# Attention block over four batches on one core: unequal maxima units, a reordered batch end, the batch loop written out

## Chip, core and metric

One core of a Trainium2 chip runs the whole program. The metric is the device time of one execution in microseconds (us); the three timed executions before the change gave 4074.82, 4076.78 and 4077.01.

## What is computed

For each of 4 batches of x (512 channels, 48 × 48 = 2304 positions, float32):

```
xn   = groupnorm(x, 32 groups) * gn_w + gn_b
qkv  = qkv_w @ xn + qkv_b            # 8 heads of 64 channels
w    = softmax((q k) / 8)            # 2304 x 2304 per head
a    = w @ v
out  = xn + proj_w @ a + proj_b
```

## The kernel before

The engines run programs of their own and meet only by semaphores. The names: `B` = 4 batches, `PAIRS` = 4 pairs of heads, `CH` = 6 chunks of `N` = 384 positions, `KT` = 18 key tiles of 128. A step is one key tile against one chunk of queries for both heads of a pair; 18 steps are a block, 108 a pair, 432 (`BSTEPS`) a batch.

**The stream.** Steps go two by two (a slot, 54 per pair, 864 in all). TensorE's `stream` (L619) issues per slot: the maxima unit of the first step, the scores of both steps (`make_scores`, L538 to 559), the maxima unit of the second, projection work for later heads (`behind`, L593), and the values products of the slot before (`make_pv`, L568). q and k are kept as a rounded part and its rest (`q_hi`, `q_lo`, ...) of type fp32r, so scores take three products; the values and the q, k, v projections are plain fp32. Scores of even steps are added onto a seed that ScalarE copies into the bank (`seed`, L759), those of odd steps onto two seed matmuls (L553); the seed is the negated row maximum.

**Maxima units.** `max_unit` (L512) makes the scores of 128 queries against 384 keys for both heads into `aux_banks`, and VectorE's `unit_max` (L860) reduces them to one number per query and head. There is one pair of banks, so each unit waits for the reduction of the one before (`aux_done`, L515). Units run `AHEAD` = 24 steps ahead of their scores. After 18 units `negate_max` (L866) reduces and turns the maxima, and SyncE's `send_max` (L353) sends them through DRAM to the seeds.

**Other engines.** ScalarE: two exponentials per slot (`exponentials`, L749), the next seed, the rounded parts. GpSimd: `add` (L1075) sums the probabilities of a block in `denom`, 17 adds a block, each waiting for the exponential and for the add before. The ring of probabilities `probs` holds `RING` = 8 steps; an exponential waits until its place was read by the values product and by the add. After a block, `finish` (L529) sums over the partitions on TensorE, VectorE's `take_recip` (L938) turns this into reciprocals in four pieces and multiplies (L961), and SyncE stores the block to `att` (`put_block`, L368).

**Order of the projection work.** `batch_plan` (L66) places the q, k, v work by hand: in the inner pairs 8 of the 9 slots of a block hold some, in the last pair 20 of 54 do, among them the next batch's first k, q and v. The next batch's x is loaded, its statistics and normalization are made in the last pair; `coefs` (L920) is a chain of small VectorE operations. The last batch has none of this.

**The end of a batch** ("seam"). TensorE ends `stream` with the last values products and the `finish` of the last block, which waits for the last add (L531). Then `projection` (L641): for each of 6 chunks, 48 matmuls of 384 columns (rounded part with both parts of the weights, then the rest), in the four score banks. `att_in` holds two chunks; `load_att` (L411) of chunk tc + 2 waits for the projection of chunk tc. ScalarE rounds a chunk (`att_high`, L743, 1536 columns), VectorE subtracts in place (`att_low`, L963), ScalarE copies each result out of the bank (L814), VectorE adds xn (L1022), SyncE stores the chunk and then loads the next x chunk into its place. `xres` and `proj_sb` lie in `probs`. The next batch's ScalarE part begins with a wait for both last stores (L840) and then seeds step 0. `batch` runs in a hardware loop (`Fori`) for batches 0 to 2; batch 3 is written out.

Of the kernel before, what the change touches and what calls it, by code (L numbers as in the profile page):

```python
# [5 lines left out]
def attention_block_program(nc, x, gn_w, gn_b, wqkv_t, bqk, bv, wproj_t, bproj, att, out):  # L6
# [17 lines left out]
    N = 384  # L24
# [21 lines left out]
    AHEAD = KT + 6  # L46
    EARLY_Q = 2
# [13 lines left out]
    NORM_AT, NORM_EVERY = 33, 2  # L61

# [101 lines left out]
    with ExitStack() as ctx:  # L164
# [27 lines left out]
        att_in = [sb(f"att_in{i}", [128, CT, N], fp32r) for i in range(2)]  # L192
# [7 lines left out]
        spare = sb("spare", [128, 1])  # L200
        small = sb("small", [128, 64])
# [12 lines left out]

        def head(e):
            return slice(e * D, (e + 1) * D)
# [9 lines left out]

        def xres(i):
            return probs[:, CT * N * i:CT * N * (i + 1)].rearrange("p (o n) -> p o n", n=N)

        proj_sb = probs[:, 2 * CT * N:4 * CT * N].rearrange("p (o n) -> p o n", n=N)  # L230
        att_hi = [buf[:, 0:CT * N].rearrange("p (k n) -> p k n", n=N)
                  for buf in (k_hi[(PAIRS - 1) % 2], k_lo[(PAIRS - 1) % 2])]
# [62 lines left out]
        def first_batch(k):  # L295
            return isinstance(k, int)
# [40 lines left out]
        def _(sp):  # L337
# [15 lines left out]
            def send_max(n, blk):  # L353


                par = blk % 2
                sp.wait_ge(neg_ready, n + 1)
                for i in range(4):
                    sp.dma_start(neg_rows[:, 32 * i:32 * (i + 1)],
                                 neg_cols[32 * i:32 * i + 2 * QT, :]).then_inc(neg_out, 16)  # L360
                sp.wait_ge(neg_out, 64 * (n + 1))
                if not isinstance(n, int) or n >= 2:
# [11 lines left out]
            def stream(b, last):  # L374
                before, _ = PLANS[last]
                nb = b + 1
                for s in range(BSTEPS):
# [18 lines left out]
                    if s in PUT_AT:  # L396
                        put_block(b, PUT_AT[s])
# [13 lines left out]
            def load_att(b, tc):  # L411
                i = tc % 2
                sp.dma_start(att_in[i][:, :, :].bitcast(fp32), att[:, :, chunk(tc)]
                             .rearrange("k c t -> c k t")).then_inc(att_back[i], 16)
# [4 lines left out]
            def projection(b):  # L419
                sp.wait_ge(att_out, PRIMED + 16 * (BLOCKS * b + BLOCKS - 1))  # L420
                load_att(b, 0)
                load_att(b, 1)
                put_block(b, BLOCKS - 1)

                for tc in range(2):
                    if tc == 1:
                        sp.wait_ge(att_out, PRIMED + 16 * BLOCKS * (b + 1))
# [36 lines left out]
            with sp.Fori(0, B - 1) as b:  # L464
                batch(b, False)
            batch(B - 1, True)
# [11 lines left out]
        def _(pe):  # L478
            mm = nc.tensor.matmul

            def bank_for(u):

                if not isinstance(u[1], int) or u[1] > 0:
                    pe.wait_ge(bank_free[u[0]], u[1])
                return bank(u)
# [26 lines left out]
            def max_unit(n, p, qt, kc):  # L512

                if not isinstance(n, int) or n > 0:
# [104 lines left out]
            def stream(b, last):  # L619
# [17 lines left out]
                finish(b, BLOCKS - 1, use(b, last, TAIL))  # L637
                if not last:
                    wait_free(pe, use(b, last, ("v", PAIRS, VG - 1)))

            def projection(b):  # L641

                pe.wait_ge(wproj_lo_ready, 1)
                for tc in range(CH):
                    i = tc % 2
                    for low in range(2):
                        pe.wait_ge(att_lo_ready if low else att_hi_ready, CH * b + tc + 1)
                        products = ([(wproj_hi, att_in[i])] if low
                                    else [(wproj_hi, att_hi[i]), (wproj_lo, att_hi[i])])
                        for ot in range(CT):  # L650
# [3 lines left out]
                            for w, a in products:  # L654
                                for k in range(CT):
                                    last = mm(scores[:, n // 2 % 2, n % 2, 0:N], w[:, k, ot * 128:(ot + 1) * 128],  # L656
                                              a[:, k, :], start=(not low and w is wproj_hi and k == 0),
                                              stop=(low == 1 and k == CT - 1))
                            if low:
                                last.then_inc(proj_full, 1)  # L660
# [39 lines left out]
            def batch(b, last):  # L700
                stream(b, last)
                projection(b)

            with pe.Fori(0, B - 1) as b:
                batch(b, False)
            batch(B - 1, True)
# [3 lines left out]
        def _(act):  # L710
# [32 lines left out]
            def att_high(b, tc):  # L743
# [3 lines left out]
                a(att_hi[i], att_in[i][:, :, :].bitcast(fp32), ACT.Copy).then_inc(att_hi_ready, 1)  # L747

            def exponentials(s, b):  # L749

                if s >= RING:
# [7 lines left out]
            def seed(s, b):  # L759
# [4 lines left out]
                if s < 2:  # L764
                    act.wait_ge(banks_opened, 1)
                    act.wait_ge(proj_saved, PRIMED + PJ * b)
# [17 lines left out]
            def stream(b, last):  # L784
                before, after = PLANS[last]
                seed(0, b)
# [16 lines left out]
                att_high(b, 0)  # L803
                save_o(b, BLOCKS - 1)

            def projection(b):
# [31 lines left out]
            def batch(b, last):  # L838
                for i in range(2):
                    act.wait_ge(stored[i], PRIMED + 16 * (CH // 2) * b)  # L840
                stream(b, last)
                projection(b)

            with act.Fori(0, B - 1) as b:
                batch(b, False)
            batch(B - 1, True)
# [3 lines left out]
        def _(dve):  # L850
# [9 lines left out]
            def unit_max(n, qt, kc, rows_negated):  # L860
# [3 lines left out]
                v.tensor_reduce(maxima[:, :, qt, kc], aux_banks[:, :, 0:N], AX.X, ALU.max).then_inc(aux_done, 1)  # L864
# [98 lines left out]
            def att_low(b, tc):  # L963

                i = tc % 2
                dve.wait_ge(att_hi_ready, CH * b + tc + 1)
                v.tensor_tensor(att_in[i][:, :, :], att_in[i][:, :, :].bitcast(fp32), att_hi[i].bitcast(fp32),
                                ALU.subtract).then_inc(att_lo_ready, 1)
# [25 lines left out]
            def stream(b, last):  # L994
# [12 lines left out]
                att_low(b, 0)  # L1007
                for piece in range(PIECES):
                    take_recip(b, BLOCKS - 1, use(b, last, TAIL), piece)

            def projection(b):
                att_low(b, 1)
# [42 lines left out]
            def batch(b, last):  # L1055
# [8 lines left out]
                projection(b)  # L1064

            with dve.Fori(0, B - 1) as b:
                batch(b, False)
            batch(B - 1, True)
# [3 lines left out]
        def _(pool):  # L1072
# [33 lines left out]
            with pool.Fori(0, B - 1) as b:  # L1106
                batch(b)
            batch(B - 1)
# [37 lines left out]
```

## Time and profile before

| | |
|---|---|
| median of three executions | 4076.78 us |
| the profiled execution | 4077.72 us, span 4076.0 us |
| mean granted TensorE clock | 0.988 |
| TensorE, VectorE, ScalarE, GpSimd busy | 97%, 54%, 57%, 74% |
| instructions | 84658 |

Times in the rows are in us from the start of the span; durations of one instruction marked ns are in nanoseconds. PE is TensorE's matmul side and PEld its weight loads, DVE is VectorE, ACT ScalarE, POOL GpSimd. A matmul's record ends where the profiler models its end, so overlapping records are a pipeline; the distance between starts is the pace. In brackets behind an instruction stand the idle time of its engine before it and what ended it.

### The profile page before, as it was taken

How to read it: one execution, taken by the hardware profiler on the slowest of the kernel's cores; microseconds unless marked ns; L12 is line 12 of the kernel's file. 1: busy time of each engine (PE TensorE's matmuls, PEld its weight loads, DVE VectorE, ACT ScalarE, POOL GpSimd, SP SyncE). 2: the span in 40 equal slices, each digit the busy share in tenths (PEclk: the TensorE clock that was granted, in tenths of full speed). 3: DMA queues.
4: the chain of work that ended last, by engine and by line, in shares of the span. 5: the costliest groups of instructions: out<-in, count | busy, mean ns of one | idle time of the engine just before them, and what ended most of it. 6: DMA issues, size and time to landing. Idle time of an engine off the chain costs nothing.

```text
span 4076.0 us, 84658 instructions
## 1 busy us (share of the span) xinstructions
PE 3933.8 (97%) x31730; PEld 2472.5 (61%) x31730; DVE 2217.9 (54%) x2809; ACT 2308.0 (57%) x3159; POOL 3004.5 (74%) x1639
## 2 busy tenths in 40 slices
PE   6999999999899999999989999999999999999997
PEld 3566665656656566565665656566567565656656
DVE  4555555565455555566545555556644555555552
ACT  2555555565455555556535555555654555555563
POOL 0778878777288888877728888887773888888893
PEclk9999999999999999999999999999999999999999
DMA  2000000120400000012130000002113000000004
GB/s 74 16 20 24 18 22 21 43 87 18 148 19 18 22 22 20 20 57 73 39 131 18 22 21 16 24 20 75 59 43 121 21 16 21 22 18 19 19 19 144
DMA packets 133751, 165.87 MB, mean 41 GB/s; under 512 B 61648, under 2 KB 110800, under 8 KB 132816
## 3 DMA queue, kind: packets, MB, share of 16 engines
q1 hardware_dynamic: 133328, 160.26, 12.5%
q8 instruction: 262, 4.29, 0.4%
q14 instruction: 161, 1.32, 0.1%
HBM read 122.17 MB, written 38.04 MB: 39 GB/s over the span
## 4 chain that ended last, share of the span: by engine, by line
PE 88%; issue 4%; DVE 3%; POOL 3%; DMA 2%; SPq 0%; ACT 0%; POOLq 0%; DVEq 0%; ACTq 0%
PE oacc L577 26%; PE scores L557 20%; PE pool_bank L495 13%; PE aux_banks L517 13%; PE pool_bank L507 7%; PE scores L656 3%; PE scores L553 3%; POOL denom L1087 3%; PE pool_bank L534 2%; DMA att_in<-att 1%; DVE maxima L864 1%; DVE turned L945 1%; DMA out<-probs 1%; PE scores L495 1%; PE scores L507 0%
## 5 line engine op out<-in xcount | busy, mean ns | idle before, releaser
L1087 POOL TENSOR_TENSOR denom<-denom,probs 128x768 f32<-128x768 f32 x1536 | 2829.3, 1842 | 568.3 <-ACT probs L756 473.3
L864 DVE TENSOR_REDUCE maxima<-aux_banks 128x2 f32<-128x768 f32 x1728 | 1657.2, 959 | 1389.1 <-PE aux_banks L517 1379.4
L756 ACT ACTIVATE probs<-scores 128x768 f32<-128x768 f32 x1728 | 1347.2, 812 | 1259.2 <-PE scores L557 1253.2
L577 PE MATMUL oacc<-probs,vals 128*64 128x384 f32 x6912 | 1277.0, 491 | 0.0
L517 PE MATMUL aux_banks<-k_hi,q_hi 64*128 64x384 f32 x3456 | 762.5, 437 | 43.2 <-DVE maxima L864 39.2
L577 PEld LDWEIGHTS oacc<-probs,vals 128*64 128x64 f32 x6912 | 471.1, 137 | 503.9 <-issue 466.8
L517 PEld LDWEIGHTS aux_banks<-k_hi,q_hi 64*128 64x128 f32 x3456 | 323.2, 184 | 693.2 <-issue 451.2
L769 ACT ACTIVATE scores<-seeds 128x768 f32<-128x768 f32 x864 | 700.1, 810 | 4.3 <-DMA out<-probs 4.3
L557 PE MATMUL scores<-q_hi,k_hi 64*128 64x384 f32 x3456 | 587.3, 335 | 22.7 <-ACT scores L769 22.6
L557 PE MATMUL scores<-q_lo,k_hi 64*128 64x384 f32 x3456 | 588.6, 335 | 0.0
L557 PE MATMUL scores<-q_hi,k_lo 64*128 64x384 f32 x3456 | 585.6, 334 | 0.0
L1084 POOL TENSOR_TENSOR denom<-probs 128x768 f32<-128x768 f32 x96 | 174.6, 1819 | 442.1 <-ACT probs L756 442.1
L557 PEld LDWEIGHTS scores<-q_hi,k_hi 64*128 64x128 f32 x3456 | 327.4, 186 | 33.9 <-ACT scores L769 32.7
L557 PEld LDWEIGHTS scores<-q_lo,k_hi 64*128 64x128 f32 x3456 | 328.0, 185 | 0.0
L557 PEld LDWEIGHTS scores<-q_hi,k_lo 64*128 64x128 f32 x3456 | 327.3, 185 | 0.0
L495 PE MATMUL pool_bank<-xn,wq 128*64 128x384 f32 x1504 | 293.2, 505 | 1.6
L553 PE MATMUL scores<-seeds,shares 64*128 64x384 f32 x1728 | 292.7, 334 | 0.0
L507 PE MATMUL pool_bank<-wv,xn 128*64 128x128 f32 x4416 | 287.9, 277 | 1.8
L495 PE MATMUL pool_bank<-xn,wk 128*64 128x384 f32 x1456 | 281.4, 501 | 1.9
L507 PEld LDWEIGHTS pool_bank<-wv,xn 128*64 128x64 f32 x4416 | 236.9, 137 | 42.9 <-issue 36.6
L553 PEld LDWEIGHTS scores<-seeds,shares 64*128 64x128 f32 x1728 | 163.2, 185 | 0.0
L495 PEld LDWEIGHTS pool_bank<-xn,wq 128*64 128x64 f32 x1504 | 90.1, 137 | 103.1 <-issue 96.8
(91 smaller groups left out, 1681.3 us busy)
## 6 DMA issues: line engine op xcount, KB each, us to landing
seeds<-neg_rows SPq DMA_DIRECT2D x96, 384.0 KB, 3.5
xtile<-x SPq DMA_DIRECT2D x72, 384.0 KB, 3.2
att<-o_norm SPq DMA_DIRECT2D x96, 192.0 KB, 1.9
att_in<-att SPq DMA_DIRECT2D x24, 768.0 KB, 6.3
probs<-x SPq DMA_DIRECT2D x24, 768.0 KB, 4.7
out<-probs SPq DMA_DIRECT2D x24, 768.0 KB, 5.2
neg_rows<-neg_cols SPq DMA_DIRECT2D x384, 0.8 KB
xn<-x SPq DMA_DIRECT2D x4, 1152.0 KB, 8.6
```

The costliest lines, as they stand in the source:

```text
L495: last = mm(to[head(e), 0:N], w[:, k, head(e)], xn[:, k, chunk(c)], start=(k == 0), stop=(k == CT - 1))
L507: last = mm(to[head(half), i * 128:(i + 1) * 128], xn[:, k, t0:t0 + D], wv[:, k, :], start=(k == 0), stop=(k == CT - 1))
L517: last = mm(aux_banks[:, e, 0:N], q_hi[head(e), qt * 128:(qt + 1) * 128], k_hi[p % 2][head(e), chunk(kc)], start=True, stop=True)
L553: mm(slot[:, e, :], shares[head(e), :], seeds[blk % 2][head(e), e * N:(e + 1) * N], start=True, stop=False)
L557: last = mm(slot[:, e, :], ks[head(e), keys], qs[head(e), queries], start=False, stop=(n == 2), skip_group_check=(s % 2 == 0))
L577: ins = mm(oacc[head(e), 0:N], vals[p % 2][:, kt, head(e)], prob(s)[:, e * N:(e + 1) * N], start=(kt == 0), stop=(kt == KT - 1))
L656: last = mm(scores[:, n // 2 % 2, n % 2, 0:N], w[:, k, ot * 128:(ot + 1) * 128], a[:, k, :], start=(not low and w is wproj_hi and k == 0), ...
L756: a(prob(s).rearrange("p (h n) -> p h n", n=N), scores[:, s % 2, :, 0:N], ACT.Exp, scale=SCALE).then_inc(probs_ready, 1)
L769: a(scores[:, 0, :, 0:N], seeds[blk % 2][:, :].bitcast(fp32).rearrange("p (e n) -> p e n", n=N), ACT.Copy).then_inc(seeded, 1)
L864: v.tensor_reduce(maxima[:, :, qt, kc], aux_banks[:, :, 0:N], AX.X, ALU.max).then_inc(aux_done, 1)
L1084: gp.tensor_tensor(acc, prob(s - 1), prob(s), ALU.add).then_inc(added, 1)
L1087: gp.tensor_tensor(acc, acc, prob(s), ALU.add).then_inc(added, 1)
```

## The change

What it does:

- The maxima units alternate between 320 and 448 keys (`UNIT_KEYS`) where they had 384 each; a slot's first unit has 320, its second 448. Their number is the same.
- `att_in` (two buffers, split in place) becomes raw, rounded and rest buffers of their own: raw chunk 0 in the x tile, raw chunk 1 new, rounded and rest of even chunks new, those of odd chunks in `k_hi` and `k_lo`.
- Chunks 0 and 1 are loaded back when block 20 of the batch is stored, chunk 2 after block 22. Chunk 0 is split in four parts of 384 columns in slots 43 to 46 (ScalarE) and 44 to 47 (VectorE) of the last pair. Later loads wait for the split of the chunk two before.
- TensorE projects chunk 0 before the last block's `finish`. ScalarE's first eight copies wait for the adds that still read their places. `proj_sb` and `xres` change places in `probs`; the x loads wait for the last add and values product.
- ScalarE seeds step 0 of the next batch between the copies of results 21 and 22; the wait for the stores moves to step 4, step 0 waits for the last output instead. A one-element exponential stands at the start of a batch.
- All engines run the four batches as a straight program.

The diff, cut to its core:

```
+    UNIT_KEYS = (320, 448)
+    SPLIT_AT = 43
...
+        def unit_keys(kc):
+            start = kc // 2 * sum(UNIT_KEYS) + kc % 2 * UNIT_KEYS[0]
+            return slice(start, start + UNIT_KEYS[kc % 2])
...
+        proj_sb = probs[:, 0:2 * CT * N].rearrange("p (o n) -> p o n", n=N)
         def xres(i):
+            return probs[:, CT * N * (2 + i):CT * N * (3 + i)].rearrange("p (o n) -> p o n", n=N)
+        att_raw = [four(xtile[:, :, :].rearrange("p a b -> p (a b)")), att_raw1[:, :, :]]
+        att_hi = [att_hi0[:, :, :], four(k_hi[last_keys])]
+        att_lo = [att_lo0[:, :, :], four(k_lo[last_keys])]
...
@@ SyncE, stream
+                        if blk == BLOCKS - 4:
+                            sp.wait_ge(xn_ready, XITEMS * (b + 1 if last else b + 2))
+                            sp.wait_ge(att_out, PRIMED + 16 * (BLOCKS * b + blk + 1))
+                            load_att(b, 0)
+                            load_att(b, 1)
+                        elif blk == BLOCKS - 2:
+                            sp.wait_ge(att_out, PRIMED + 16 * (BLOCKS * b + blk + 1))
+                            load_next_att(b, 0)
...
+            def load_next_att(b, tc):
+                sp.wait_ge(att_lo_ready, CT * (CH * b + tc + 1))
+                load_att(b, tc + 2)
@@ SyncE, projection
-                sp.wait_ge(att_out, PRIMED + 16 * (BLOCKS * b + BLOCKS - 1))
-                load_att(b, 0)
-                load_att(b, 1)
-                put_block(b, BLOCKS - 1)
+                sp.wait_ge(pv_done, PRIMED + BSTEPS * (b + 1))
+                sp.wait_ge(added, PRIMED + ADDS * BLOCKS * (b + 1))
                 for tc in range(2):
                     sp.dma_start(xres(tc), chan(x, b, tc)).then_inc(xres_in[tc], 16)
                 for tc in range(CH):
-                    if tc + 2 < CH:
-                        sp.wait_ge(proj_full, PJ * b + CT * (tc + 1))
-                        load_att(b, tc + 2)
+                    if tc == 2:
+                        sp.wait_ge(att_out, PRIMED + 16 * BLOCKS * (b + 1))
+                    if tc + 3 < CH:
+                        load_next_att(b, tc + 1)
+                    if tc == 0:
+                        put_block(b, BLOCKS - 1)
@@ TensorE
-                    last = mm(aux_banks[:, e, 0:N], q_hi[head(e), qt * 128:(qt + 1) * 128],
-                              k_hi[p % 2][head(e), chunk(kc)], start=True, stop=True)
+                    last = mm(aux_banks[:, e, 0:UNIT_KEYS[kc % 2]], q_hi[head(e), qt * 128:(qt + 1) * 128],
+                              k_hi[p % 2][head(e), unit_keys(kc)], start=True, stop=True)
...
                 for tc in range(CH):
+                    if tc == 1:
+                        finish(b, BLOCKS - 1, use(b, last, TAIL))
@@ ScalarE
             def exponentials(s, b):
+                if s == 0:
+                    act.wait_ge(out_ready, PRIMED + PJ * b)
+                if s == RING // 2:
+                    for i in range(2):
+                        act.wait_ge(stored[i], PRIMED + 16 * (CH // 2) * b)
...
+                    n = i - (PAIRS - 1) * SLOTS - SPLIT_AT
+                    if 0 <= n < CT:
+                        att_high(b, 0, slice(n, n + 1))
...
+                    else:
+                        act.wait_ge(added, PRIMED + ADDS * BLOCKS * (b + 1) - (RING - 1 - n // 2))
                     a(proj_sb[:, n % 8, :], ...
+                    if n == PJ - 3 and not last:
+                        seed(0, b + 1, PRIMED + PJ * b + n + 1)
...
             def batch(b, last):
-                for i in range(2):
-                    act.wait_ge(stored[i], PRIMED + 16 * (CH // 2) * b)
+                a(warm[:, :], ones[:, 0:1], ACT.Exp)
@@ VectorE, stream
+                    n = i - (PAIRS - 1) * SLOTS - SPLIT_AT - 1
+                    if 0 <= n < CT:
+                        att_low(b, 0, slice(n, n + 1))
@@ every engine
-            with pe.Fori(0, B - 1) as b:
-                batch(b, False)
-            batch(B - 1, True)
+            for b in range(B):
+                batch(b, b == B - 1)
```

## Rows read from the trace of the kernel before

**Rows 1.** The page, part 1: busy us (share of span) xinstructions.

```profile
PE 3933.8 (97%) x31730; PEld 2472.5 (61%) x31730; DVE 2217.9 (54%) x2809; ACT 2308.0 (57%) x3159; POOL 3004.5 (74%) x1639
```

**Rows 2.** Windows, two pairs: stretch, us, PE, PEld, DVE, ACT, POOL busy, PEclk, DMA.

```profile
563.00:793.00 230.00, 229.72 (x1910) 140.27 (x1908) 127.56 (x157) 136.05 (x186) 187.40 (x102) 1.00 0.07 20
3341.60:3572.20 230.60, 229.78 (x1910) 141.09 (x1910) 127.70 (x157) 132.87 (x187) 187.14 (x102) 1.00 0.07 20
```

**Rows 3.** Time line, batch 3, slot without projection work: start us, us.

```profile
3930.20 0.18 PEld L517 LDWEIGHTS aux_banks<-k_hi,q_hi 64*128 64x128 f32 x2 [0.60 <-DVE maxima L864]
...
3930.69 0.96 DVE L864 TENSOR_REDUCE maxima<-aux_banks 128x2 f32<-128x768 f32 x1 [0.86 <-PE aux_banks L517]
...
3931.29 1.51 ACT L756 ACTIVATE probs<-scores 128x768 f32<-128x768 f32 x2 [1.09 <-PE scores L557]
...
3931.36 0.19 PEld L557 LDWEIGHTS scores<-q_lo,k_hi 64*128 64x128 f32 x2
3931.53 0.34 PE L557 MATMUL scores<-q_lo,k_hi 64*128 64x384 f32 x2
3931.70 0.19 PEld L517 LDWEIGHTS aux_banks<-k_hi,q_hi 64*128 64x128 f32 x2 [0.16 <-DVE maxima L864]
...
3932.07 1.51 PE L577 MATMUL oacc<-probs,vals 128*64 128x384 f32 x8
3932.18 0.96 DVE L864 TENSOR_REDUCE maxima<-aux_banks 128x2 f32<-128x768 f32 x1 [0.54 <-PE aux_banks L517]
...
3932.70 0.81 ACT L769 ACTIVATE scores<-seeds 128x768 f32<-128x768 f32 x1
...
3933.51 0.19 PEld L517 LDWEIGHTS aux_banks<-k_hi,q_hi 64*128 64x128 f32 x2 [0.60 <-DVE maxima L864]
```

**Rows 4.** Time line of the first seam, and the last batch's end.

```profile
1040.28 1.55 PE L534 MATMUL pool_bank<-denom,ones 128*64 128x384 f32 x4 [4.38 <-POOL denom L1087]
...
1098.27 0.44 PE L517 MATMUL aux_banks<-k_hi,q_hi 64*128 64x384 f32 x2 [0.94 <-ACT probs L814]
...
1103.98 1.28 ACT L769 ACT_TABLE_LOAD   x1 [6.04 <-DMA out<-probs]
...
4015.84 1.55 PE L534 MATMUL pool_bank<-denom,ones 128*64 128x384 f32 x4 [12.13 <-POOL denom L1087]
```

**Rows 5.** Windows, after the first seam, and the last projection.

```profile
1106.10:1110.50 4.40, 4.36 (x22) 3.11 (x24) 0.96 (x1) 2.33 (x3) 0.81 (x1) 0.50 0.00 0
4022.10:4070.80 48.70, 48.40 (x275) 47.28 (x273) 19.32 (x27) 18.09 (x28) 0.00 (x0) 1.00 0.71 239
```

**Rows 6.** Time line of TensorE in the last slots of batch 3, without units.

```profile
3997.43 0.35 PE L557 MATMUL scores<-q_lo,k_hi 64*128 64x384 f32 x2
...
3997.72 1.51 PE L577 MATMUL oacc<-probs,vals 128*64 128x384 f32 x8
...
4000.64 0.34 PE L557 MATMUL scores<-q_lo,k_hi 64*128 64x384 f32 x2
...
4000.91 0.54 PE L577 MATMUL oacc<-probs,vals 128*64 128x384 f32 x2
```

**Rows 7.** By source line: duration ns min/median/max, start of first, last.

```profile
L869 DVE TENSOR_REDUCE neg_max<-maxima x96: 190/191/192, 86.9 to 3958.3; 128x6 fp32r<-128x36 f32 x96
L961 DVE TENSOR_TENSOR o_norm<-o_raw,recip x96: 547/1360/2223, 159.9 to 4018.9; 128x384 f32<-128x384 f32 x96
```

**Rows 8.** Time line of GpSimd, in the loop and in batch 3.

```profile
568.48 3.73 POOL L1087 TENSOR_TENSOR denom<-denom,probs 128x768 f32<-128x768 f32 x2 [2.04 <-ACT probs L756]
...
3929.89 5.78 POOL L1087 TENSOR_TENSOR denom<-denom,probs 128x768 f32<-128x768 f32 x3
```

**Rows 9.** Time line, a product L961 in a slot without projection work.

```profile
3890.55 2.11 DVE L961 TENSOR_TENSOR o_norm<-o_raw,recip 128x384 f32<-128x384 f32 x1
...
3893.58 0.44 PE L517 MATMUL aux_banks<-k_hi,q_hi 64*128 64x384 f32 x2 [0.92 <-DVE maxima L864]
```

**Rows 10.** The page, DMA issues: out<-in, count, KB each, us to landing.

```profile
out<-probs SPq DMA_DIRECT2D x24, 768.0 KB, 5.2
```

More of the change, by code:

```diff
@@ L191, in attention_block_program @@
         wproj_lo = sb("wproj_lo", [128, CT, C], fp32r)
-        att_in = [sb(f"att_in{i}", [128, CT, N], fp32r) for i in range(2)]
+        att_hi0 = sb("att_hi0", [128, CT, N], fp32r)
+        att_lo0 = sb("att_lo0", [128, CT, N], fp32r)
+        att_raw1 = sb("att_raw1", [128, CT, N])
         groups = sb("groups", [128, 128])
@@ L481, in bank_for @@
             def bank_for(u):
-                if not isinstance(u[1], int) or u[1] > 0:
+                if u[1] > 0:
                     pe.wait_ge(bank_free[u[0]], u[1])
@@ L636, in stream, with projection @@
                 make_pv(BSTEPS - 1, b, last)
[L637 to L641, printed above, removed]
+            def projection(b, last):
                 pe.wait_ge(wproj_lo_ready, 1)
@@ L645, in projection @@
                     i = tc % 2
+                    if tc == 1:
+                        finish(b, BLOCKS - 1, use(b, last, TAIL))
+                        if not last:
+                            wait_free(pe, use(b, last, ("v", PAIRS, VG - 1)))
                     for low in range(2):
-                        pe.wait_ge(att_lo_ready if low else att_hi_ready, CH * b + tc + 1)
-                        products = ([(wproj_hi, att_in[i])] if low
+                        pe.wait_ge(att_lo_ready if low else att_hi_ready, CT * (CH * b + tc + 1))
+                        products = ([(wproj_hi, att_lo[i])] if low
                                     else [(wproj_hi, att_hi[i]), (wproj_lo, att_hi[i])])
@@ L655, in projection @@
                                 for k in range(CT):
-                                    last = mm(scores[:, n // 2 % 2, n % 2, 0:N], w[:, k, ot * 128:(ot + 1) * 128],
-                                              a[:, k, :], start=(not low and w is wproj_hi and k == 0),
-                                              stop=(low == 1 and k == CT - 1))
+                                    ins = mm(scores[:, n // 2 % 2, n % 2, 0:N], w[:, k, ot * 128:(ot + 1) * 128],
+                                             a[:, k, :], start=(not low and w is wproj_hi and k == 0),
+                                             stop=(low == 1 and k == CT - 1))
                             if low:
-                                last.then_inc(proj_full, 1)
+                                ins.then_inc(proj_full, 1)
             pe.sem_inc(pv_done, PRIMED)
@@ L701, in batch @@
                 stream(b, last)
-                projection(b)
-            with pe.Fori(0, B - 1) as b:
-                batch(b, False)
-            batch(B - 1, True)
+                projection(b, last)
+            for b in range(B):
+                batch(b, b == B - 1)
         @block.scalar
@@ L757, in exponentials, with seed @@
                   scale=SCALE).then_inc(probs_ready, 1)
-            def seed(s, b):
+            def seed(s, b, since=None):
                 blk = s // KT
@@ L765, in seed @@
                     act.wait_ge(banks_opened, 1)
-                    act.wait_ge(proj_saved, PRIMED + PJ * b)
+                    act.wait_ge(proj_saved, since)
                 else:
@@ L838, in batch @@
             def batch(b, last):
-                for i in range(2):
-                    act.wait_ge(stored[i], PRIMED + 16 * (CH // 2) * b)
+                a(warm[:, :], ones[:, 0:1], ACT.Exp)
                 stream(b, last)
[L842 to L846, printed above, removed]
+                projection(b, last)
+            act.wait_ge(consts_made, 5)
+            seed(0, 0, PRIMED)
+            for b in range(B):
+                batch(b, b == B - 1)
         @block.vector
@@ L1063, in batch @@
                 stream(b, last)
[L1064 to L1068, printed above, removed]
+                projection(b, last)
+            for b in range(B):
+                batch(b, b == B - 1)
         @block.gpsimd
@@ L1104, in batch @@
                     add(s, b)
-            with pool.Fori(0, B - 1) as b:
+            for b in range(B):
                 batch(b)
-            batch(B - 1)
 def kernel(**inputs):
```

48 lines of the change are left out of this document (22 added, 26 removed).

## The prediction, made before the change was run

> **What bounds the kernel now.** The page first: TensorE is busy in 97% of the span [rows 1], so time can only come from what stands between its matmuls. Then the windows, one pair of heads each: in 230.6 us of an undisturbed pair it is busy 229.8 [rows 2]. It looks full, but a matmul that waits for its weights counts as busy, so the time line of one pair of steps has to be read [rows 3], a "slot" from here on. It holds two maxima units (L517), two score steps and two steps of values, 3.31 us in all. The second unit's weight load starts at 3931.70, 0.05 after the reduction of the first unit ends (3930.69 + 0.96). Other loads start 0.17 ahead of their matmul, as the one at 3931.36 for 3931.53 does; the unit's would have started at about 3931.53. So VectorE's reduction of unit one is late by 0.17 us for the load, and part of that shows on TensorE. Last I read the ends of the batches: windows and time line of the seam [rows 4, 5].
>
> **Units of 320 and 448 keys.** From the last scores pair to the first values pair there are 0.54 us with a unit between (3931.53 to 3932.07) [rows 3]; without one it is 0.29 and 0.27 [rows 6]. A unit's pair itself takes 0.17, so 0.08 to 0.10 are lost per slot; I take 0.09. The reduction takes 0.96 us for 768 values [rows 3] and 0.191 for 36 [rows 7], 1.05 ns a value. An estimate by that slope: 0.83 for 640 values, 1.09 for 896. The first unit's matmuls also end 0.03 sooner (64 of 384 columns of 0.17). Together 0.16 of the missing 0.17: the load is back in its place to 0.01. The total of columns stays the same. Bounds: below nothing if the reduction does not shrink with its width, 0.17 at most, the whole lateness.
> What is late next is unit one of the next slot, behind the reduction of 896. In the slot without projection work the reduction now ends at 3932.18 + 0.96 = 3933.14, the load starts at 3933.51 [rows 3]: 0.37 spare, of which 0.05 is the signal. The new reduction is 0.13 longer, its matmuls end 0.03 later but start 0.09 sooner, and the slot is 0.09 shorter: some 0.17 stays. ScalarE's chain is as close: exp, exp, seed from 3931.29 to 3933.51 [rows 3], and the scores behind unit one want the seed about 0.1 after 3933.51. At most this eats some of the 0.09 in slots without projection work, one in nine in the inner pairs.
> How many slots: 12 inner pairs of 54 are 648; the last pairs of batches 0 to 2 add 162; the last pair of batch 3 counts with its first 9 only, since GpSimd bounds the rest. 819 × 0.09 = 74 us.
> The Trainium skill (TensorE: Matmul & The Clock Gate, Part 3, The mechanism) has it that a weight load overlaps a running matmul only where the row groups differ; both halves are in use by the scores in front, so by that rule the 0.09 would stay. That is rival A, 4028 us in full. The trace speaks against it: loads on the same halves run 0.17 ahead all through the slot.
>
> **Straight program.** Batch 3 already is one, and its pair takes 230.6 us by the windows against 230.0 and a little in the loops (the windows are cut at tenths; I take 0.45 more in the straight one), with the same work [rows 2]. 9 pairs × 0.45 = +4 us. GpSimd loses more: two adds in the loop span 3.73, three in the straight batch 5.78 [rows 8]; with 1.83 each (half of 3.73 less the gap) the gap goes from 0.08 to 0.14. 17 adds then take 33.5 us against 37.5 of a block: hidden. But VectorE's product L961, two inputs from SBUF, takes 1.36 in the median and 0.55 at least [rows 7]; I read the difference as the wait until an add is over. GpSimd loses its 0.2 of idle time a slot, so the product may end up to 0.2 later, with about 0.1 left until it delays unit one's reduction. 96 blocks × 0 to 0.1, taken as +5 us.
>
> **The seam.** TensorE stops at 1035.90 (1040.28 − 4.38, waiting for the sums) and makes its first scores at 1106.1, when the table load at 1103.98 and the seed behind it (0.81) are over [rows 4]: 70.2 us. In the new order projection chunk 0 follows at once, its data split before the end; the sums' finish stands behind it. Its matmuls go at 48.40/275 = 0.176 us with the missing records [rows 5], so 288 take 50; the finish 0.65 at full clock. A chunk is 8.3 us, GpSimd's lag about 4.3 + 1 (its wider gaps) + 1 (less TensorE time): just covered; without this cover TensorE waits for it behind chunk 0. Then unit one waits for the last copy, 0.9 after the last matmul group began to end [rows 4], + 0.7 since the next seed (0.81) now stands in ScalarE's queue before the last two copies, + 0.3 to the scores. 52.5 us against 70.2: 17.7. The loads of the attention chunks now wait for the split of the chunk two before, not for its projection, so their landing and split are hidden behind 8.3; SyncE passes a store and its 5.2 us [rows 10] before each, which still fits. The x loads start later, at the sums' end, and the outputs with them; 8 buffers of results take that up. Stores (ScalarE's 6.04 wait at 1103.98) are now waited for at step 4, some 8 us into the batch, where they are hidden; the table load of 1.28 goes too [rows 4]. Where batch 3 begins that load is absent already: 1.3 less. So 17.7 × 3 − 1.3 = 52 us. The clock: behind the idle time the granted clock was 0.50, half of 2.4 GHz, in 1106.1 to 1110.5 [rows 5], 2.2 us lost; without a pause it should stay up, 3 × 2 = 6 us. Seams: 58 us.
>
> **Added before the seam.** The split of chunk 0 is now four copies and four subtractions in the last slots, which have no projection work. ScalarE has 1.09 us idle in each [rows 3], a copy needs half of that. The subtraction, of the form of L961, does not fit: in such a slot L961 took 2.11 and TensorE lost 0.92 [rows 9]. 4 × 3 batches × 0.75 = +9 us (0 to 13). In the last batch no units run there any more. SyncE's new waits at the 21st and 23rd block are for work done some ten steps before; the row maxima queued behind them are sent more than 20 steps ahead of their use.
>
> **The last seam.** TensorE waits 12.13 us for the sums, until 4015.84 [rows 4], and GpSimd's chain is unchanged. Chunk 0 (8.3) now runs in that wait: −8. The program's first seed, too, needs no table load (1.28): −1.
>
> **Sum.** −74 + 4 + 5 − 58 + 9 − 8 − 1 = −123. The profiled execution took 4077.7 us (span 4076.0), 0.9 over the median: 4077.7 − 123 − 0.9 = 3954 us.
>
> **Rivals.**
> A. The units give nothing: load not pulled ahead, or ScalarE's chain paces. For: every unit load of [rows 3] waits, none shows the other case. Against: the scores loads. 3954 + 74 = 4028 in full; half, 3991. Chance 0.12.
> B. The seam is not bound by matmuls: SyncE's queue (x load, attention load, store, wait) paces it as now, 1 to 2 us per chunk, or the sums come late behind chunk 0. 3 × 8 = 24 us back: 3978. For: one queue carries all of it. Against: each load has a chunk's time more. Chance 0.12.
> C. Slower. The reduction of 896 holds unit one in every slot. It decides from 0.17 us beyond my 1.09 in bare slots, about 0.8 in the others. To turn 123 − 8 us it would have to cost 0.15 to 0.2 in each of 852 slots, so take some 2 us: 4077 + 10 = 4087. Against: the slope of [rows 7]. Chance 0.02.
> D. The product of L961 slips by a whole add in each block: up to 0.92 [rows 9] × 72 = 66 us, 4020. Chance 0.06.
> The forecast itself has 0.68. Its own range is 3930 to 3975: 0.08 to 0.10 per slot (±8), the subtractions (−9, +4), L961 (±5), seams ±6.
>
> **How the numbers follow.** The likeliest case gives 3954. The range takes in B and half of A: 3925 to 3992; outside are full A, C, D and a little luck below. About 0.2% (8 us) can be told from no change. Faster 0.96, same 0.02, slower 0.02.
>
> **What would show it.** The window of an inner pair at 225 to 226 us; the load of the second unit 0.17 ahead of its matmul, and 0.27 to 0.29 from unit to values; reductions of 0.83 and 1.09; GpSimd's gaps 0.14 everywhere; 52 to 54 us from the last values to the next scores, granted clock 1.00 across; a table load only around the square roots and before the first exponential. It is wrong if the pair stays at 230, if TensorE waits for attention data within a seam, or if unit one waits for the wide reduction.

## The result, and the profile after

The changed kernel takes 3937.84 us in the median of four runs (3936.28 to 3938.25), against 4076.9 for the kernel before: a ratio of 0.9657 (95% interval 0.9641 to 0.9674), 139 us less. The forecast was 3954 us, in a range of 3925 to 3992.

The page of the changed kernel, part 1, against [rows 1]: TensorE's share rises by one point only, but for the same 31730 matmuls it is busy for 3842.4 us where it was 3933.8: a matmul that waits for its weights counts as busy. With equal units and all else changed (below) it is 3919.1, so 77 of these 91 us go with the units.

```profile
PE 3842.4 (98%) x31730; PEld 2451.3 (62%) x31730; DVE 2223.0 (56%) x2821; ACT 2275.7 (58%) x3173; POOL 3002.6 (76%) x1639
```

Windows of an inner pair after, in the columns of [rows 2]: 225.0 us where it was 230, for the same instructions.

```profile
1200.00:1425.00 225.00, 224.63 (x1912) 139.58 (x1910) 127.58 (x157) 132.98 (x187) 187.25 (x103) 1.00 0.07 21
```

The time line of a slot without projection work, batch 3, against [rows 3]:

```profile
3756.27 0.19 PEld L546 LDWEIGHTS aux_banks<-k_hi,q_hi 64*128 64x128 f32 x2 [0.60 <-DVE maxima L904]
...
3756.73 0.83 DVE L904 TENSOR_REDUCE maxima<-aux_banks 128x2 f32<-128x640 f32 x1 [0.56 <-PE aux_banks L546]
...
3757.34 1.51 ACT L791 ACTIVATE probs<-scores 128x768 f32<-128x768 f32 x2 [1.01 <-PE scores L586]
...
3757.41 0.19 PEld L586 LDWEIGHTS scores<-q_lo,k_hi 64*128 64x128 f32 x2
...
3757.58 0.34 PE L586 MATMUL scores<-q_lo,k_hi 64*128 64x384 f32 x2
3757.61 0.19 PEld L546 LDWEIGHTS aux_banks<-k_hi,q_hi 64*128 64x128 f32 x2
3757.76 0.36 PE L546 MATMUL aux_banks<-k_hi,q_hi 64*128 64x448 f32 x2
...
3758.05 1.51 PE L606 MATMUL oacc<-probs,vals 128*64 128x384 f32 x8
3758.16 1.09 DVE L904 TENSOR_REDUCE maxima<-aux_banks 128x2 f32<-128x896 f32 x1
...
3758.75 0.82 ACT L804 ACTIVATE scores<-seeds 128x768 f32<-128x768 f32 x1
...
3759.48 0.19 PEld L546 LDWEIGHTS aux_banks<-k_hi,q_hi 64*128 64x128 f32 x2 [0.60 <-DVE maxima L904]
```

The first reduction (640 values) takes 0.83 us and ends at 3757.56, the load follows 0.05 later, at 3757.61, 0.15 ahead of its matmuls at 3757.76. The matmuls keep the pace of the scores (3757.58 to 3757.76), and the values follow after 0.29 where it was 0.37, though this pair is 64 columns wider. The slot takes 3.21 us, not 3.31. The load is still released by the reduction: counted over the 852 slots that hold units, the second unit's load starts 0.05 us behind the reduction's end in the median, in the changed kernel as before, and 0.15 behind it in the kernel with 256 keys first (below). It is only no longer late enough to matter.

Windows of the first seam and of its edge, against [rows 5], and the time line, against [rows 4]:

```profile
1011.00:1067.00 56.00, 54.54 (x316) 51.70 (x318) 25.66 (x33) 22.97 (x33) 8.92 (x5) 1.00 0.62 200
1066.30:1075.00 8.70, 7.45 (x58) 4.55 (x60) 5.78 (x11) 5.04 (x8) 3.65 (x2) 1.00 0.37 133
```

```profile
1013.62 0.96 PE L686 MATMUL scores<-att_hi,wproj_hi 128*128 128x384 f32 x4
...
1022.14 0.87 PE L563 MATMUL pool_bank<-denom,ones 128*64 128x384 f32 x4
...
1061.09 7.40 SPq L465 DMA_DIRECT2D out<-probs  x2
...
1061.89 2.94 PE L686 MATMUL scores<-k_lo,wproj_hi 128*128 128x384 f32 x16
...
1064.45 0.81 ACT L804 ACTIVATE scores<-seeds 128x768 f32<-128x768 f32 x1 [0.39 <-ACT probs L852]
...
1066.29 0.42 PE L546 MATMUL aux_banks<-k_hi,q_hi 64*128 64x320 f32 x2 [1.46 <-ACT probs L852]
...
1066.54 0.33 PE L586 MATMUL scores<-q_hi,k_hi 64*128 64x384 f32 x2
...
1068.12 1.51 ACT L791 ACTIVATE probs<-scores 128x768 f32<-128x768 f32 x2 [1.79 <-DVE probs L1065]
```

Chunk 0 starts as the last values product ends, the finish (L563) stands behind it without a wait, and the scores start at 1066.54: 52.9 us from the end of the values (1013.69) where it was 70.2. The granted clock is 1.00 over both windows. The last two stores land 7.40 us after 1061.09; nothing waits for them. The first exponential waits 1.79 us for VectorE's last output, whose x chunk comes late. TensorE has its first scores by then, but the reduction of the first unit stands behind that output too, and the second unit waits for it:

```profile
1069.20 0.47 PE L546 MATMUL aux_banks<-k_hi,q_hi 64*128 64x448 f32 x2 [1.25 <-DVE maxima L904]
```

Time line of the last seam, and the window over it. Chunk 0 ends and the finish still waits for GpSimd, 2.88 us by the row where it was 12.13 [rows 4]; the granted clock stays at 1.00 in this execution.

```profile
3881.48 2.94 PE L686 MATMUL scores<-att_lo,wproj_hi 128*128 128x384 f32 x16
...
3887.30 0.87 PE L563 MATMUL pool_bank<-denom,ones 128*64 128x384 f32 x4 [2.88 <-POOL denom L1129]
```

```profile
3884.00:3892.00 8.00, 5.12 (x29) 4.20 (x28) 1.95 (x4) 2.29 (x3) 3.10 (x2) 1.00 0.44 138
```

### The profile page after: what moved, and what is told of

Read it like the earlier page. It is cut to its first block, busy times and chain, and to the rows that moved or that the text cites. A ratio compares the mean times of both kernels' runs of the same rounds, so it can differ in the third digit from the quotient of the medians.

```text
span 3936.0 us, 77117 instructions
## 1 busy us (share of the span) xinstructions
PE 3842.4 (98%) x31730; PEld 2451.3 (62%) x31730; DVE 2223.0 (56%) x2821; ACT 2275.7 (58%) x3173; POOL 3002.6 (76%) x1639
## 4 chain that ended last, share of the span: by engine, by line
PE 66%; POOL 4%; DVE 2%; DMA 1%; issue 1%; ACT 0%; POOLq 0%; SPq 0%; DVEq 0%; ACTq 0%
PE oacc L606 20%; PE scores L586 16%; PE pool_bank L524 10%; PE aux_banks L546 8%; PE pool_bank L536 5%; POOL denom L1129 3%; PE scores L582 3%; PE scores L686 2%; PE pool_bank L563 1%; DMA out<-probs 1%; DVE maxima L904 1%; DMA probs<-x 0%; ACT probs L791 0%; DVE probs L1065 0%; DVE att_lo L1008 0%
## 5 line engine op out<-in xcount | busy, mean ns | idle before, releaser
L904 DVE TENSOR_REDUCE maxima<-aux_banks 128x2 f32<-128x640 f32 x1728 | 1657.9, 959 | 1318.3 <-PE aux_banks L546 1288.9
L791 ACT ACTIVATE probs<-scores 128x768 f32<-128x768 f32 x1728 | 1310.8, 810 | 1247.3 <-PE scores L586 1231.2
L546 PE MATMUL aux_banks<-k_hi,q_hi 64*128 64x448 f32 (+1 forms) x3456 | 683.4, 391 | 41.2 <-DVE maxima L904 35.0
```

The lines of the kernel that those rows point to most:

```text
L546: last = mm(aux_banks[:, e, 0:UNIT_KEYS[kc % 2]], q_hi[head(e), qt * 128:(qt + 1) * 128], k_hi[p % 2][head(e), unit_keys(kc)], start=True, ...
L791: a(prob(s).rearrange("p (h n) -> p h n", n=N), scores[:, s % 2, :, 0:N], ACT.Exp, scale=SCALE).then_inc(probs_ready, 1)
L904: v.tensor_reduce(maxima[:, :, qt, kc], aux_banks[:, :, 0:UNIT_KEYS[kc % 2]], AX.X, ALU.max)\
```

## The experiments

All times are medians of four or more runs; kernels of one group ran on the same chip with the kernel before, which gave 4078.25, 4079.76 and 4079.88 us in the three groups.

### Equal units in the changed kernel

```
-    UNIT_KEYS = (320, 448)
+    UNIT_KEYS = (384, 384)
```

> The changed kernel with equal units (384 and 384) again, all else changed. Theory: a slot loses the 0.10 us that the trace after shows regained (0.697 + 0.542 against 0.667 + 0.470), in some 810 slots: 3938 + 83 = 4021 us, inner pairs back at 230.2, the second unit's load 0.17 behind the last scores matmul. Rival (the straight program, with waits on constants, brings most of the pair's gain): 3945 to 3960 us, pairs at 226.

Measured: 4015.8 us (ratio 0.9845, 0.9828 to 0.9861). Inner pair, in windows:

```profile
551.00:781.70 230.70, 229.88 (x1910) 141.16 (x1908) 127.79 (x156) 132.99 (x187) 187.23 (x103) 1.00 0.07 20
```

The units are worth 4015.8 − 3936.7 = 79 us; the second number is the changed kernel in the second group, which ran on another chip (the kernel before differs by 1.5 us between the two). The rival falls.

### Unequal units in the kernel before

```
+    UNIT_KEYS = (320, 448)
-    last = mm(aux_banks[:, e, 0:N], q_hi[...], k_hi[p % 2][head(e), chunk(kc)], ...)
+    last = mm(aux_banks[:, e, 0:UNIT_KEYS[kc % 2]], q_hi[...], k_hi[p % 2][head(e), unit_keys(kc)], ...)
-    v.tensor_reduce(maxima[:, :, qt, kc], aux_banks[:, :, 0:N], ...)
+    v.tensor_reduce(maxima[:, :, qt, kc], aux_banks[:, :, 0:UNIT_KEYS[kc % 2]], ...)
```

> The kernel before, with units of 320 and 448 keys alone. Theory: inner pairs at 224.9 in the loops too, 4077 - 83 = 3994 us, seams as before (70 us). Rival (the units need the other parts): less than half of it, above 4035 us.

Measured: 3999.04 us (ratio 0.9803, 0.9787 to 0.9820), 79 us again, in loops:

```profile
551.00:775.50 224.50, 224.50 (x1912) 138.87 (x1910) 127.50 (x157) 136.07 (x187) 187.82 (x103) 1.00 0.07 21
```

The gain does not depend on the rest, and the pair is 0.5 us shorter than in the changed kernel. TensorE is busy in all of it.

### The straight program alone

```
-            with pe.Fori(0, B - 1) as b:
-                batch(b, False)
-            batch(B - 1, True)
+            for b in range(B):
+                batch(b, b == B - 1)
```
(on every engine; `first_batch(k)` becomes `k == 0`)

> The kernel before, with the four batches written out alone. Theory as predicted: pairs 230.2 to 230.6 (up to +4 us in sum), two table loads of 1.3 us and the branch fewer at the seams: 4074 to 4079 us, no change that can be told; GpSimd's gaps 0.14 in all batches. Rival (the 16 us by which the result beat the forecast come from here): 4058 to 4065 us.

Measured: 4074.43 us (ratio 0.9991, 0.9981 to 1.0000), 3.8 us less than the kernel before of its group. Its inner pairs take 230.7 us, 0.5 more, as forecast (9 × 0.5 = +4.5); its later seams 67.6 and 67.5 from values to scores where they took 70.0 and 68.8 before. One more thing differs: once a batch, in batches 0 to 2, TensorE stands behind the chain of small VectorE operations of `coefs`, for 5.64 to 5.68 us before and for 3.80 here and 3.84 in the changed kernel.

```profile
867.25 0.69 PE L517 MATMUL aux_banks<-k_hi,q_hi 64*128 64x384 f32 x2 [5.64 <-DVE maxima L864]
```

In this kernel:

```profile
866.25 0.69 PE L516 MATMUL aux_banks<-k_hi,q_hi 64*128 64x384 f32 x2 [3.80 <-DVE maxima L861]
```

GpSimd's two adds, against [rows 8]:

```profile
567.81 3.80 POOL L1083 TENSOR_TENSOR denom<-denom,probs 128x768 f32<-128x768 f32 x2 [2.06 <-ACT probs L754]
```

3.80 − 3.73 = 0.07 us more between two adds. The longer pairs and the shorter seams nearly cancel.

### 448 keys first

```
-    UNIT_KEYS = (320, 448)
+    UNIT_KEYS = (448, 320)
```
(and the first units wait for one k chunk more)

> The changed kernel with the order of widths turned: 448 first, 320 second. Theory (the first unit's reduction prices the slot, one to one once it is late): against equal units the first reduction is 0.13 us longer and its matmuls end 0.03 later, so 0.16 more in each of some 810 slots: 4021 + 130 = 4151 us, pairs at 238.9. Rival (the width matters little; the balance of both units counts): within 15 us of equal units, 4010 to 4035 us.

Measured: 4128.62 us (ratio 1.0122, 1.0105 to 1.0139). The time line of units and reductions:

```profile
1300.46 0.47 PE L546 MATMUL aux_banks<-k_hi,q_hi 64*128 64x448 f32 x2
...
1300.98 1.09 DVE L904 TENSOR_REDUCE maxima<-aux_banks 128x2 f32<-128x896 f32 x1 [0.37 <-PE aux_banks L546]
...
1302.12 0.41 PE L546 MATMUL aux_banks<-k_hi,q_hi 64*128 64x320 f32 x2
...
1302.58 0.83 DVE L904 TENSOR_REDUCE maxima<-aux_banks 128x2 f32<-128x640 f32 x1 [0.51 <-PE aux_banks L546]
```

Between the units there are 1.66 us, where 1.49 stand in the changed kernel (3756.27 to 3757.76). A pair takes 238.0 us, 7.3 over equal units: 0.135 a slot, not 0.16. The theory forgot that the second unit's matmuls then are 0.027 shorter; 0.16 − 0.027 = 0.13. Late widths are priced one to one, and the order alone moves the kernel by 192 us.

### 256 and 512 keys

```
-    UNIT_KEYS = (320, 448)
+    UNIT_KEYS = (256, 512)
```

> The changed kernel with units of 256 and 512 keys. Theory: the first reduction is early enough with 320 already, so nothing more is won there, and the wide reduction (1024 values, 1.23 us) still ends before unit one's load, whose spare falls from 0.18 to about 0.03 us: 3938 us, within 4. Rival (rival C of the prediction: the wide reduction holds unit one in slots without projection work, and there the products behind it hurt more): 3945 us or more.

Measured: 3935.18 us (ratio 0.9646, 0.9629 to 0.9663), the changed kernel within the noise. By source line, the reductions of this kernel:

```profile
L904 DVE TENSOR_REDUCE maxima<-aux_banks x1728: 628/956/1229, 43.1 to 3823.6; 128x2 f32<-128x512 f32 x96, 128x2 f32<-128x1024 f32 x96
```

They now last up to 1.229 us, and inner pairs take 224.7 instead of 224.9. Time line of the first reduction and the second unit's load:

```profile
3755.15 0.69 DVE L904 TENSOR_REDUCE maxima<-aux_banks 128x2 f32<-128x512 f32 x1
...
3755.99 0.19 PEld L546 LDWEIGHTS aux_banks<-k_hi,q_hi 64*128 64x128 f32 x2
```

The load is 0.17 ahead of its matmuls (3756.16) and 0.15 behind the reduction's end, so it no longer waits for it. The pair is 0.3 us shorter than with 320 keys, 0.005 a slot, for the last 0.03 of lateness. So 320 was early enough. Behind the wide reduction no first unit is held, here or in the changed kernel: past the program's start the load of none follows the reduction's end by less than 0.06 us. Rival C's mechanism has no price even at 1024 values.

### The changed kernel again

As the reference for the second group:

> The changed kernel itself, as the reference of this group. 3938 us again, within 0.1%.

Measured: 3936.68 us (ratio 0.9649, 0.9633 to 0.9665).

### The split of chunk 0 six slots earlier

```
-    SPLIT_AT = 43
+    SPLIT_AT = 37
```

> The changed kernel with the four-part split of chunk 0 six slots earlier (slots 37 to 41), of which all but one hold projection work. Theory: the subtractions no longer delay unit one's reduction, so the last pairs of batches 0 to 2 shorten by what the split costs, forecast 3 us each, by the trace rather 2: 3938 - 6 = 3932 us. Rival (the split is hidden as it is): 3938 us.

Measured: 3933.93 us (3931.70 to 3935.99) against 3936.68 (3935.24 to 3938.31) for the changed kernel in the same group: 2.8 us, hardly clear of the spread. Time line of the changed kernel in slots 44 to 47:

```profile
980.61 0.80 DVE L1008 TENSOR_TENSOR att_lo<-xtile,att_hi 128x384 fp32r<-128x384 f32 x1
...
983.84 1.66 DVE L1008 TENSOR_TENSOR att_lo<-xtile,att_hi 128x384 fp32r<-128x384 f32 x1
...
986.29 0.48 PE L546 MATMUL aux_banks<-k_hi,q_hi 64*128 64x448 f32 x2 [0.48 <-DVE maxima L904]
...
987.82 1.75 DVE L1008 TENSOR_TENSOR att_lo<-xtile,att_hi 128x384 fp32r<-128x384 f32 x1
...
990.36 0.47 PE L546 MATMUL aux_banks<-k_hi,q_hi 64*128 64x448 f32 x2 [0.59 <-DVE maxima L904]
...
991.88 1.73 DVE L1008 TENSOR_TENSOR att_lo<-xtile,att_hi 128x384 fp32r<-128x384 f32 x1
```

Two of the four subtractions delay the next unit by 0.48 and 0.59 us, and by 0.45 to 0.59 in batches 1 and 2. In the earlier slots no unit behind them has such a wait in these three batches. In the last batch, where slots 37 to 41 still hold units, two have, of 0.58 and 2.66 us; the pair, which GpSimd bounds, takes 198.0 us all the same, between the 199.1 and 197.0 of the changed kernel's two executions. Time line of the last batch, earlier split:

```profile
3824.95 2.16 DVE L1008 TENSOR_TENSOR att_lo<-xtile,att_hi 128x384 fp32r<-128x384 f32 x1
...
3827.90 0.47 PE L546 MATMUL aux_banks<-k_hi,q_hi 64*128 64x448 f32 x2 [2.66 <-DVE maxima L904]
```

The last pairs of batches 0 to 2 are 3.6 us shorter in sum than in the changed kernel of the group; more than that was forecast (6) and is not there.

### The split in one piece at the end

```
-                    n = i - (PAIRS - 1) * SLOTS - SPLIT_AT
-                    if 0 <= n < CT:
-                        att_high(b, 0, slice(n, n + 1))
+                att_high(b, 0)
                 save_o(b, BLOCKS - 1)
```
(the same on VectorE; chunk 2 is then loaded at the seam)

> The changed kernel with chunk 0 split in one piece behind the last slot. Theory: TensorE has nothing to project for 1.5 (rounding) behind its last values and wants the rest 5.5 us later, which takes 3 us: the pause is 0 to 1 us only, because ScalarE's rounding starts before the last values end, and the 2 us a seam that the four parts cost are saved: 3935 to 3938 us. Rival (the early split is what makes the seam gapless): 4 to 6 us a seam more, 3955 us.

Measured: 3936.20 us (ratio 0.9652, 0.9634 to 0.9669). The seam keeps its length, 52.7 us from values to scores. ScalarE rounds before the last values end and VectorE is done before the rest is wanted:

```profile
1010.35 1.48 ACT L774 ACTIVATE att_hi<-xtile 128x1536 fp32r<-128x1536 f32 x1
...
1011.93 2.02 DVE L1004 TENSOR_TENSOR att_lo<-xtile,att_hi 128x1536 fp32r<-128x1536 f32 x1 [1.08 <-ACT att_hi L774]
```

The four parts bring nothing here.

### The next seed and the wait for the stores back at the head

```
-                    if n == PJ - 3 and not last:
-                        seed(0, b + 1, PRIMED + PJ * b + n + 1)
...
             def batch(b, last):
                 a(warm[:, :], ones[:, 0:1], ACT.Exp)
+                for i in range(2):
+                    act.wait_ge(stored[i], PRIMED + 16 * (CH // 2) * b)
+                if b > 0:
+                    seed(0, b, PRIMED + PJ * b)
```
(and the wait at step 4 goes)

> The changed kernel with the next batch's first seed and the wait for both last stores back at the head of the batch. Theory: TensorE's first scores wait for the stores again, some 5 to 6 us after the last output, and the granted clock falls behind the pause (2 us more): 6 to 8 us per seam, 3938 + 21 = 3959 us. Rival (the store was not what the seam waited for): under 3945 us.

Measured: 3954.95 us (3953.55 to 3958.74), 18 us over the changed kernel of the group, 6 a seam. The time line:

```profile
1070.83 0.81 ACT L801 ACTIVATE scores<-seeds 128x768 f32<-128x768 f32 x1 [5.36 <-DMA out<-probs]
...
1071.69 0.69 PE L586 MATMUL scores<-q_hi,k_hi 64*128 64x384 f32 x2 [5.85 <-ACT scores L801]
```

ScalarE waits 5.36 us for a store, TensorE 5.85 for the seed. 4.4 to 5.2 us more lie between values and scores, 14 of the 18 us in sum. The rest goes with the clock, which is 0.50 in the window from 1071.7 to 1076.4: the matmul behind the pause takes 0.69 us, as in the trace before, where it takes 0.33 at full clock (1066.54 above).

### The finish ahead of chunk 0

```
-                    if tc == 1:
+                    if tc == 0:
                         finish(b, BLOCKS - 1, use(b, last, TAIL))
```

> The changed kernel with the finish of the last block ahead of chunk 0 again. Theory: TensorE waits for the sums, 6 us at each of three seams and 12 at the end, where chunk 0 hid them; the granted clock falls to 0.5 behind the pause as in the trace before, 2 to 3 us each: 3938 + 3 x 8 + 10 = 3972 us. Rival (the sums' lag is given back, since the outputs go on at the pace of the stores): 3945 to 3955 us.

Measured: 3971.71 us (3970.92 to 3972.82), 35 us over the changed kernel. Time line and window of the first seam:

```profile
1020.06 1.55 PE L563 MATMUL pool_bank<-denom,ones 128*64 128x384 f32 x4 [6.74 <-issue]
```

```profile
1020.00:1025.20 5.20, 5.14 (x15) 3.99 (x16) 1.95 (x4) 0.00 (x0) 0.00 (x0) 0.50 0.77 250
```

TensorE stands still for 6.74 us, then the granted clock is 0.50 (1.2 GHz) for the next 5.2. From values to scores there are 61.9, 62.0 and 61.4 us, 9 more in each of three seams; the end of the program, from the last values on, is 8 us longer than in the changed kernel of the group. This one order is worth more than half of all that the reordering gives.

### Sums of two or three steps on TensorE in the last pair

On top of the earlier split, in blocks 1 to 5 of the last batch's last pair:

```
+    LIGHT = (10, 14)              # second kernel: (8, 11, 14)
@@ TensorE, make_pv
+                if is_light(s, b):
+                    u = use(b, last, ('finish', p, blk % CH))
+                    to = bank_for(u) if kt == LIGHT[0] else bank(u)
+                    for e in range(2):
+                        mm(to[head(e), 0:N], ones[:, :], prob(s)[:, e * N:(e + 1) * N],
+                           start=(kt == LIGHT[0]), stop=False)
@@ GpSimd, add
+                if is_light(s, b):
+                    pool.wait_ge(added, PRIMED + ADDS * (BLOCKS * b + blk) + kt - 1)
+                    pool.sem_inc(added, 1)
+                    return
```
(the finish then adds to these sums)

> The changed kernel with the split of chunk 0 in slots 37 to 41 and, in blocks 1 to 5 of the last batch's last pair, the sums of two steps (10 and 14 of 18) made by TensorE (two matmuls against ones, added to what the finish gives) and not by GpSimd. Theory: that pair is bound by GpSimd, 17 adds of 1.97 us a block; 15 take 29.6 and TensorE's block is 30 to 31, so 2.5 us a block and the 4 to 7 us of waiting behind chunk 0 go: 3934 - 16 = 3918 us. Rival (TensorE or ScalarE bound that pair already): 3934 + 6 = 3940 us.

> As the one before, with three steps of 18 (8, 11, 14) on TensorE. Theory: GpSimd then needs 27.6 us and TensorE is the bound, 0.65 us more in each of five blocks: 3 us over the version with two, 3921 us. Rival (GpSimd is the bound still with two): 3910 us or less.

Measured: 3928.86 us with two steps (ratio 0.9630, 0.9613 to 0.9647) and 3925.62 with three (ratio 0.9623, 0.9606 to 0.9640; 3924.37 to 3927.31). Windows of the last 141 us of the stream of the changed kernel, and of a like stretch with three steps:

```profile
3735.00:3876.00 141.00, 129.60 (x973) 76.17 (x972) 65.08 (x79) 89.51 (x124) 131.37 (x72) 0.96 0.11 35
```

```profile
3725.00:3870.00 145.00, 141.54 (x1081) 84.24 (x1080) 69.84 (x84) 93.00 (x128) 115.60 (x63) 1.00 0.12 37
```

GpSimd goes from 131.4 busy in 141 us to 115.6 in 145, TensorE from 92% to 98%. The wait behind chunk 0 is gone in both; it was 4.06 us with the earlier split alone, and 2.88 and 5.19 in the two executions of the changed kernel. But the last pair shortens only from 198.0 (earlier split alone) to 197.8 and 195.5, not by 2.5 us a block: the gain of the two-step version lies at the end, which is 5.4 us shorter. Why is not shown. Two things bear on it: the added matmuls take TensorE's time, and the earlier subtraction of chunk 0 still holds a unit, for 2.66 us with two steps (3823.95) and for 1.15 with three (3821.94). Three steps are the fastest kernel here, 11 us under the changed one. Four were not tried.

## Why the prediction was right

The range held and so did the mechanisms of its two large terms, the units and the order at the seams. The total was 16 us too cautious; the units, the product and the split are each some 5 us of that, the last seam 2 to 4. Term by term:

**Units**: −74 forecast, −79 measured twice. The slope of the reduction held (0.83 and 1.09 us), and of the lateness of 0.17 there stays 0.03 (3757.61 against 3757.58), where I had 0.01. The step was 0.09 a slot. Like against like, the inner pairs show 5.7/54 = 0.106: 230.65 with equal units against 224.9, and 230.2 against 224.4 in loops. The count of slots was too high in return. From the profiled execution with equal units to that of the changed kernel the twelve inner pairs take 68 us less (648 × 0.09 = 58 forecast), the last pairs of batches 0 to 2 take 10 less (162 × 0.09 = 15), and that of batch 3 0.3 less. So the sum is nearer than its parts. The rule of the Trainium skill (TensorE: Matmul & The Clock Gate, Part 3, The mechanism) that a load overlaps a running matmul only on other row groups did not hold here: the load at 3757.61 runs during the matmuls begun at 3757.58, on the same halves. Rival A is out.

**Straight program**: +4 for the pairs is what the pairs of the straight program alone show (+0.5 each). In total that kernel was 3.8 us below its kernel before, so the rest of it gained about 8. In the profiled executions the three seams are 3.9 shorter, the last pairs of the batches 2.6, and the way from the program's first scores to its first exponential 1.2 (4.22 to 3.04); the end is 1.2 longer. The shorter pause behind `coefs`, 5.6 us in three batches, lies within those last pairs, which gain less than that; why it is shorter was not tested. I had counted the seams' part within the seam term, as a new length.

**The product, now L1002** (L961 before): +5 forecast, nothing measured. The pair of 224.9 is explained by 224.4 in the loop and 0.5 for the straight program. The product is tied to an add as before: all 87 products of more than 0.6 us end 0.41 to 0.42 us behind the end of an add, in both kernels. They take 1.31 us in the median, no longer than the 1.36 of [rows 7]; GpSimd's lost idle time did not move them. By source line, the changed kernel:

```profile
L1002 DVE TENSOR_TENSOR o_norm<-o_raw,recip x96: 550/1310/1607, 156.7 to 3889.7; 128x384 f32<-128x384 f32 x96
```

**Split before the seam**: +9 forecast, some 3 to 5 measured: 2.8 us by moving it; in the kernel with the split in one piece the last pairs are 1.2 to 2.2 us shorter, though its total does not show that. The step that was off is the 0.75 us for each of four: only two held a unit, by 0.48 and 0.59. The first subtraction took just 0.80 us. GpSimd was in an unbroken run of adds, but this one ran across the end of an add (981.00) and the gap up to the next (981.14).

**Seam**: 52.5 us forecast, 52.6 to 52.9 measured, and the clock at full speed across. All but the units and the straight program is worth 4074.4 − 4015.8 = 59 us; the forecast for it was −58 + 9 − 8 − 1 = −58. The sum was right, its parts less so. From the profiled execution of the straight program alone to that with equal units, in us: seams −47.0, which with the 3.9 of the straight program makes 51 (52 forecast); the first pairs of the batches with the way from first scores to first exponential −4.1 (6 forecast, for the clock); the end −12.4 (8 forecast); last pairs of batches 0 to 2 +4.1 (9 forecast), of batch 3 +1.6 (nothing forecast); before the first scores −0.5.

**Last seam**: −8 forecast; from the last values to the last projection matmul it took 66.98 us before and 54.17 after, 58.54 in the second execution of the changed kernel, whose last pair was 2.1 us shorter. Pair and end together are 12 and 10 us shorter than before. The term that I left out is the clock. Behind the wait of 12.13 it was 0.51 in the window from 4015.8 to 4022.1, and behind the wait of 2.88 it stayed at 1.00. In the second execution the wait was longer and the clock did fall, as its row and window show:

```profile
3886.49 1.55 PE L563 MATMUL pool_bank<-denom,ones 128*64 128x384 f32 x4 [5.19 <-POOL denom L1129]
```


```profile
3884.10:3890.90 6.80, 4.41 (x13) 3.23 (x14) 1.95 (x4) 0.00 (x0) 2.19 (x2) 0.51 0.46 144
```

Rivals B to D did not come. Attention data were never waited for by TensorE within a seam, though one queue carries them; the sums come late behind chunk 0 (the other half of B) only at the last seam; the wide reductions hold no first unit (C), and the product did not slip (D).

## What to carry to other kernels

A matmul counts as busy while its weights are late, so an engine at 99.6% can still hide a wait per step: compare the start of a weight load with the start of the matmul before it. Where two pieces of work share one buffer with unequal time behind each, cut them unequally, the small one where the time is short; the wrong order cost 113 us over equal units here, the right one gained 79. At a stage's end, work whose data are ready belongs ahead of work that waits for the slowest engine, and a pause costs its own length and, in most of those seen here, the slow clock behind it.

## What was not expected

- A weight load late by 0.03 us (3757.61, with the matmul before at 3757.58) costs some 0.005 us a slot, by 0.17 us it cost 0.10.
- The straight program's inner pairs take 0.5 us longer than the loop's with the same work, and GpSimd's gap between dependent adds is 0.07 us longer. Why was not tested.
- The length of a wait does not by itself tell what the clock does. Waiting 2.88 us (3887.30) left the granted clock at 1.00. In the same execution it was 0.50 behind a wait of 2.90, as the row and window below show, and 0.50 behind the wait of 3.84 that `coefs` still causes once a batch (848.0 to 851.1). That wait is TensorE's longest pause left behind the start of the program.

```profile
3785.06 0.87 PE L563 MATMUL pool_bank<-denom,ones 128*64 128x384 f32 x4 [2.90 <-POOL denom L1129]
```

```profile
3786.70:3790.00 3.30, 3.30 (x18) 1.99 (x16) 2.15 (x4) 2.33 (x3) 3.01 (x3) 0.50 0.00 0
```
